# A two-layer decoder on one core: another order of the opening, filler products, casts on ScalarE, later clears, the last scaling on VectorE

## The chip, the cores and the metric

The kernel runs on one core of a Trainium2 chip, as one launch. The metric is the device time of an execution in microseconds; less is better. A core has five instruction queues: TensorE (PE: products and transposes), VectorE (DVE), ScalarE (ACT), GpSimd (POOL) and SyncE (SP, which here only issues transfers). Each works off its own list in order, and they wait for each other through semaphores.

## The reference, cut to what matters

The input x has shape (4, 512, 128), a context (4, 154, 128). Six blocks follow each other, each with a residual and a layer norm behind it:

```python
x = _layernorm(x + _L0_attn_ref(x, ...))        # 16 heads of 8, causal; q and k are layer-normed
x = _layernorm(x + _L0_xattn_ref(x, ctx, ...))  # 16 heads of 8 over the context
x = _layernorm(x + _L0_ffn_ref(x, ...))         # 8 experts, softmax gates of at least 0.1
x = _layernorm(x + _L1_attn_ref(x, ...))        # linear attention, chunks of 128
x = _layernorm(x + _L1_xattn_ref(x, ctx, ...))  # 8 heads of 128 over the context
x = _layernorm(x + _L1_ffn_ref(x, ...))         # gated, 384 hidden
```

The start of the first block is what the edits touch most: `qkv = x @ W_qkv`, q and k each normed over their 128 features (mean and variance), then scores q.k per head, a maximum per row, the exponentials.

## The kernel before, in words

The work is cut by batch (b = 0 to 3). A batch passes two "attention" blocks in turns of four heads (`TURNS`, line 78 on): a turn makes the scores `S` (the causal ones in five pieces), VectorE takes their maxima (`maxima`, L1783 and L1788), which are split into bf16 parts (L1800 to L1806), transposed (`mT`) and written by SyncE as extra rows beside q (L798); then the transposed scores `ST`, their exponentials on ACT (L1537) and the products with v (`PV`). The four blocks behind it (`rest_groups`) work on halves of a batch (h = 0, 1), in buffers called slots: z = 0 and 1 for batches 0 to 2, z = 2 and 3 for batch 3. Batches overlap: attention of one runs beside the rest of the one before.

Scores are exact to about f32 because q and k are split into three bf16 parts each (`parts`, first, second, third: rounded value, rounded remainder, remainder of that) and placed by transfers six times, each into rows of the 64-row contraction ("placing", `place_self`, L777 on SyncE; for the first batch half of them on ACT, `place_first`, L1457). The placings with third parts are all among ACT's. K and Q buffers (`Q6`, `K6`) must have been cleared before, which POOL does by memsets (L884 to L901): for batch 0 first, then K_1 (for cross attention), then, in `late_zeros`, the halves for batch 1, and VXR and vaug.

All engines walk one list of steps, `schedule()`. 16 streams of steps are merged by a written-out string, `MERGE`, one letter for each step or group; `BANK_OF` gives the PSUM bank of each step that needs one. Each engine does its part of a step, in the order of the list, so a step that stands earlier in the list stands earlier in each engine's queue. `takes` and `held_back` say which steps must stand ahead of which.

The steps of the opening, for a batch: `x0T` transposes x (L1051), ACT copies it (L1444); `qkv` makes four products of 128x384 (L1082), ACT copies each (L1485); `qk_moments` on VectorE (L1715, L1723); `qk_norm`: POOL takes the root of the variances (`root`, L945 and L948), then for batch 0 VectorE scales q (L1735) and ACT k (L1492), for later batches POOL both (L913); `qkT` transposes q, then k, ACT writes the first part (L1507), VectorE the remainder `left` (L1759), the second part (L1749) and the third (L1751); `place`. `wT` steps transpose the context and weights of later blocks. `xv` makes the values of the cross attention; VectorE adds their bias (L1882, L1887).

The norms of the rest: VectorE makes the moments (L1827, L1831), POOL the root and, in `shifted` (L953), minus mean times root; ACT scales (`norm`, L1663); step `store` sends the result out (L809).

## Time and profile before

| | |
|---|---|
| median of 3 runs | 491.82 us (491.47 to 494.59) |
| the profiled execution | 493.74 us |
| its span, first to last instruction | 491.9 us |
| busy, PE / DVE / ACT / POOL | 458.1 / 384.5 / 351.2 / 190.2 us |
| mean granted TensorE clock | 0.984 of full speed |

Busy times of the engines overlap. A row of the timeline or of the chain gives the start and the length in microseconds; "issue" is time in which an engine waited for nothing that the profile shows, among it the landing of transfers. The granted clock is given as a share of 2.4 GHz; 0.50 is 1.2 GHz. In the shares by line, PE has 74% of the chain that ended last and DVE 9%.

### The profile page before, as it was taken

To read this page: it belongs to the slowest core of one execution; us is meant where nothing else is said; L and a number is where in the kernel's file an instruction comes from. 1 tells how busy PE (TensorE), PEld (TensorE's weight loads), DVE (VectorE), ACT (ScalarE), POOL (GpSimd) and SP (SyncE) were. 2 spreads that over 40 slices of the span, in tenths; PEclk is the share of its full clock that TensorE was granted. 3 is DMA by queue.
4 is the path that set the end of the run, shared out by engine and by line. 5 is a ranking of instruction groups with operands and counts; after the bars stand their busy time and mean duration, and the time that the engine had idled before them with its cause. 6 is when DMAs were issued, how large, how long until landed. Compare 5 with 4: busy or idle time off the path is not lost.

```text
span 491.9 us, 12390 instructions
## 1 busy us (share of the span) xinstructions
PE 458.1 (93%) x4416; PEld 307.2 (62%) x4416; DVE 384.5 (78%) x1133; ACT 351.2 (71%) x893; POOL 190.2 (39%) x365
## 2 busy tenths in 40 slices
PE   5567989998999999999999999999999999999994
PEld 2344557655546546666778555658754756996894
DVE  3559998799899999997788888858788678554465
ACT  3326676866858769887776688986767878969743
POOL 8760001570101644344143232334414537646352
PEclk9689999999999999999999999999999999999999
DMA  7650310032300213001110000030000000000001
GB/s 240 152 148 4 105 31 25 4 86 73 88 4 23 66 39 85 17 2 26 35 35 21 6 3 2 4 88 4 2 13 13 0 2 1 1 2 1 1 1 43
DMA packets 27185, 18.40 MB, mean 37 GB/s; under 512 B 8217, under 2 KB 26773, under 8 KB 26997
## 3 DMA queue, kind: packets, MB, share of 16 engines
q1 hardware_dynamic: 23413, 15.44, 11.8%
q10 hardware_dynamic: 3712, 2.17, 1.7%
q8 instruction: 36, 0.59, 0.5%
q14 instruction: 24, 0.20, 0.1%
HBM read 5.58 MB, written 1.05 MB: 13 GB/s over the span
## 4 chain that ended last, share of the span: by engine, by line
PE 74%; DVE 9%; POOL 6%; issue 3%; ACT 3%; DMA 2%; SPq 2%; ACTq 0%; POOLq 0%; DVEq 0%
PE psum L1051 11%; PE psum L1372 6%; PE psum L1162 6%; PE psum L1395 6%; PE psum L1308 6%; PE psum L1103 5%; PE psum L1130 4%; DVE nmax L1788 4%; PE psum L1406 4%; PE psum L1152 3%; PE psum L1149 3%; PE psum L1417 2%; PE psum L1190 2%; PE psum L1082 2%; PE psum L1109 1%
## 5 line engine op out<-in xcount | busy, mean ns | idle before, releaser
L1537 ACT ACTIVATE EX<-psum 128x1024 f32<-128x1024 f32 (+1 forms) x128 | 118.5, 976 | 8.7 <-PE psum L1136 4.3
L1788 DVE TENSOR_REDUCE nmax<-psum 128x2 f32<-128x768 f32 (+1 forms) x96 | 77.5, 861 | 7.4 <-PE psum L1109 7.2
L1783 DVE TENSOR_REDUCE nmax<-psum 128x4 f32<-128x616 f32 (+1 forms) x80 | 68.1, 876 | 2.9 <-PE psum L1103 2.6
L1103 PE MATMUL psum<-K,Q 64*128 64x154 bf16 (+4 forms) x512 | 50.9, 268 | 5.9 <-issue 4.5
L1014 POOL TENSOR_TENSOR GP<-REST,xrs 128x512 f32<-128x512 f32 (+1 forms) x48 | 32.5, 700 | 41.4 <-DVE xrs L2025 27.6
L1130 PE MATMUL psum<-Q,K 64*128 64x512 bf16 (+3 forms) x320 | 44.7, 315 | 1.6 <-DVE nmax L1788 1.2
L1620 ACT ACTIVATE REST<-psum,nxmax 128x154 f32<-128x154 f32 x96 | 36.2, 395 | 10.7 <-DVE nxmax L2015 9.8
L1444 ACT COPY pvraw<-psum 128x512 f32<-128x512 f32 x32 | 18.7, 585 | 34.3 <-PE psum L1162 24.6
L1103 PEld LDWEIGHTS psum<-K,Q 64*128 64x128 bf16 x512 | 21.4, 95 | 28.2 <-issue 19.1
L1162 PE MATMUL psum<-EX,V 128*32 128x256 f32 (+3 forms) x512 | 37.8, 435 | 0.1
L945 POOL TENSOR_SCALAR rstd_rest<-moments_rest 128x2 f32<-128x2 f32 x32 | 7.3, 228 | 79.1 <-DVE moments_rest L1831 78.7
L2015 DVE TENSOR_REDUCE nxmax<-psum 128x2 f32<-128x308 f32 x64 | 28.7, 469 | 5.8 <-PE psum L1372 5.1
L1372 PE MATMUL psum<-GP,xT 128*128 128x308 f32 x96 | 30.3, 431 | 0.0
L1109 PE MATMUL psum<-maskS,ident 64*128 64x64 bf16 (+1 forms) x512 | 28.3, 207 | 0.0
L1109 PEld LDWEIGHTS psum<-maskS,ident 64*128 64x128 bf16 x512 | 23.8, 97 | 6.5
L1136 PE MATMUL psum<-maskT,ident 64*128 64x64 bf16 (+1 forms) x512 | 27.2, 203 | 0.0
L1136 PEld LDWEIGHTS psum<-maskT,ident 64*128 64x128 bf16 x512 | 22.9, 94 | 6.2
L1162 PEld LDWEIGHTS psum<-EX,V 128*32 128x32 f32 x512 | 14.5, 109 | 18.0 <-issue 16.9
L1395 PE MATMUL psum<-VM,REST 128*128 128x128 f32 x192 | 24.1, 278 | 0.3
L948 POOL TENSOR_TENSOR rstd_rest<-rstd_rest,power 128x2 f32<-128x2 f32 x32 | 22.9, 714 | 2.7
L926 POOL COPY V<-qkn 128x256 f32<-128x256 f32 x8 | 3.7, 461 | 51.9 <-PE psum L1162 51.9
L1395 PEld LDWEIGHTS psum<-VM,REST 128*128 128x128 f32 x192 | 22.4, 192 | 1.7 <-issue 1.1
(338 smaller groups left out, 1162.4 us busy)
## 6 DMA issues: line engine op xcount, KB each, us to landing
Q<-xparts SPq DMA_DIRECT2D x24, 128.0 KB
Q<-parts SPq DMA_DIRECT2D x21, 128.0 KB
K<-parts SPq DMA_DIRECT2D x21, 128.0 KB
X<-in_x SPq DMA_DIRECT2D x4, 256.0 KB, 3.6
Q<-in_L_xattn_Wkv SPq DMA_DIRECT2D x1, 1024.0 KB, 6.6
K<-xkparts SPq DMA_DIRECT2D x24, 38.5 KB
out<-XB_rest SPq DMA_DIRECT2D x6, 128.0 KB, 1.9
Q<-in_L_xattn_Wq SPq DMA_DIRECT2D x1, 512.0 KB, 4.4
```

The lines of the kernel that those rows point to most:

```text
L1051: last = nc.tensor.transpose(to[0:n, at:at + m], src, ident[0:m, 0:m])
L1103: last = mm(to[:, r, at:at + n], Q6[a][p, b % 2, 2 * g + jj, P * q:P * q + P], K6[a][p, b % 2, 2 * g + jj, 0:n], start=True, stop=bool(a))
L1109: last = mm(to[:, r, at + n - P + TILE * e:at + n], ident2[p, e, :], maskS[p, e, TILE * e:P], start=False, stop=e == 0)
L1130: last = mm(to[:, r, at:at + n], K6[a][p, b % 2, 2 * g + jj, P * k:P * k + P], Q6[a][p, b % 2, 2 * g + jj, P * k:S], start=True, stop=bool(a))
L1136: last = mm(to[:, r, at:at + TILE * (e + 1)], ident2[p, e, :], maskT[p, e, 0:TILE * (e + 1)], start=False, stop=e == 1)
L1162: last = mm(to[32 * h:32 * h + 32, P * k:S], V[:, k, 4 * g + h, :], EX[:, ex_slot(b, a, g, u) + h % 2, at:at + n], start=k == PV_ORDER[0], ...
L1372: fills_(mm(fill(key)[:, 0:2 * C], half_of(b, h).xT[4][:, P * q:P * q + P], G[:, head:head + 2, :].rearrange("p h c -> p (h c)")), key)
L1395: mm(to, of.XPT[:, head, :], VM[:, head, :], start=head == 0, stop=False)
L1537: drains(nc.scalar.activation(dst, src, ACT.Exp), key)
L1620: last = nc.scalar.activation(of.XE[:, i, :], src[:, C * j:C * j + C], ACT.Exp, bias=of.nxmax[:, i:i + 1], accum_out=of.xsum[:, i:i + 1])
L1783: last = vec.tensor_reduce(nmax[:, :, :, q], src[:, :, 0:2 * n].rearrange("p r (j k) -> p r j k", j=2), AX.X, ALU.max, negate=True)
L1788: last = vec.tensor_reduce(nmax[:, :, jj, q], src[:, :, at:at + P * (q + 1)], AX.X, ALU.max, negate=True)
```

## The change

What it does, part by part:

- The first product of the second batch must stand behind the last placing of the first (`takes`). `MERGE` and `BANK_OF` are new throughout: most steps move by a few places. Of the `wT` steps none stands ahead of the first scores any more, `xv` stands behind the scores of the fourth turn instead of ahead of those of the second.
- ACT makes the second parts of q and k for batch 0; for this the two remainders have buffers of their own, `left` and a piece of EX.
- POOL's clears of K_1 and its late clears stand behind the second batch's scalings.
- TensorE multiplies the identity by itself, six times ahead of the first transposes of x and twice ahead of the first qkv product; nothing reads the results.
- For batch 3 `shifted` is left out behind the root, and VectorE makes (Y - mean) * root in place of ACT, four times for each half.

```diff
@@ takes @@
     if what == "qkv":
-        return [(b, "x0T", 0)]
+        return [(b, "x0T", 0)] + ([(0, "place", 1, 1)] if b == 1 else [])
@@ MERGE: the order of the steps, by stream @@
-    "rrrrrrwurrrrwllrlruuurrlrsssssuuuuvsssusuttsstrrttsssspptssttttllpsssrpptsslltttstpu"
+    "rrrrrrrrrwrlwlllrrrsrrssuuuussruuuuuusssststtsrttssspptstststlrptsssspwplllttststtvu"
...
@@ BANK_OF: the PSUM bank of each step @@
-    "024613570246135062406234523046270460246250624064206245064206420624016247024602460123"
+    "024613570246124067160234523640264062046124602460246702402640642064523064204602460123"
...
@@ build @@
+        def first_left(w):
+
+            return EX[:, 0, :] if w else left[:, :]
@@ gpsimd @@
             pool.wait_ge(first_zeros_ready, 1)
-            step(nc.gpsimd.memset(words(K6[1].rearrange("p b h t -> p (b h) t")), 0.0))
-            step(nc.gpsimd.memset(K6[1].rearrange("p b h t -> p (b h) t").bitcast(F32)[
-                :, :, 0:C // 2], TWO_ONES))
 
             def late_zeros():
-                pool.wait_ge(qk_normed, 1)
+                step(nc.gpsimd.memset(words(K6[1].rearrange("p b h t -> p (b h) t")), 0.0))
+                step(nc.gpsimd.memset(K6[1].rearrange("p b h t -> p (b h) t").bitcast(F32)[
+                    :, :, 0:C // 2], TWO_ONES))
                 for w, value in enumerate((0.0, TWO_ONES)):
                     step(nc.gpsimd.memset(words((Q6, K6)[w][0][:, 1, :, :]), value))
@@ qk_norm @@
                 if b == 0:
-                    late_zeros()
                     return
...
                     last.then_inc(qk_normed, 1)
+                if b == 1:
+                    late_zeros()
@@ rest_root @@
-                step(root(of.rstd, of.moments, LN_EPS))
-                shifted(of.shift, of.moments, of.rstd, 2).then_inc(rest_rstd_ready[z], 1)
+                last = root(of.rstd, of.moments, LN_EPS)
+                if b < B - 1:
+                    step(last)
+                    last = shifted(of.shift, of.moments, of.rstd, 2)
+                last.then_inc(rest_rstd_ready[z], 1)
@@ tensor @@
+            def keep_busy(to, count):
+
+                for _ in range(count):
+                    mm(to[:, 0:P], ident[:, :], ident[:, :], start=True, stop=True)
@@ x_T @@
                 if n == 0:
+                    if b == 0:
+                        keep_busy(fill((0, "x0T", 0)), 6)
                     pe.wait_ge(x_loaded[b], 16)
@@ qkv @@
+                key = (b, "qkv", n)
                 if n == 0:
+                    if b == 0:
+                        keep_busy(fill(key), 2)
                     drained(pe, (b, "x0T", 0))
                     if b == 0:
                         pe.wait_ge(wqkv_ready, 1)
-                key = (b, "qkv", n)
@@ scalar: qkT @@
+                if b == 0 and w:
+                    for v in range(2):
+                        drained(act, (0, "qkT", v))
+                        copy(parts[:, v, 1, :], first_left(v)).then_inc(part_ready[0][1], 1)
@@ scalar: norm @@
+                if b == B - 1:
+                    return
                 z, of = slot(b, a), half_of(b, a)
@@ vector: qkT @@
-                drains(vec.scalar_tensor_tensor(left[:, :], bank(key),
+                rest = first_left(w) if b == 0 else left[:, :]
+                drains(vec.scalar_tensor_tensor(rest, bank(key),
                                                 col("k_scale") if w else col(QS),
                                                 parts[:, w, 0, :], ALU.mult, ALU.subtract), key)
-                drained(dve, key)
-                split(left[:, :], parts[:, w, :, :], part_ready[0], 2 * b + w + 1)
+                if b:
+                    drained(dve, key)
+                    split(rest, parts[:, w, :, :], part_ready[0], 2 * b + w + 1)
+                elif w:
+                    for v in range(2):
+                        dve.wait_ge(part_ready[0][1], v + 1)
+                        vec.tensor_tensor(parts[:, v, 2, :], first_left(v), parts[:, v, 1, :],
+                                          ALU.subtract).then_inc(part_ready[0][2], 1)
+                    splits.append((part_ready[0][2], 2))
@@ vector @@
-            work = {"qk_moments": qk_moments, "qk_norm": qk_norm, "qkT": qkT,
+            def last_norm(b, h, n=None):
+
+                if n is None or b < B - 1:
+                    return
+                z, of = slot(b, h), half_of(b, h)
+                dve.wait_ge(rest_rstd_ready[z], norms_until(b, n))
+                dst = of.XB if n == 5 else of.X[n + 1]
+                for i in range(2):
+                    last = vec.tensor_scalar(dst[:, i, :], of.Y[:, i, :], of.moments[:, i, 0:1],
+                                             of.rstd[:, i:i + 1], ALU.subtract, ALU.mult)
+                last.then_inc(rest_x_ready[z], 1)
+
+            work = {"norm": last_norm, "qk_moments": qk_moments, "qk_norm": qk_norm, "qkT": qkT,
```
The names in the rows of order are those of buffers; a number behind x is how many of a kind follow each other. ACT in the opening before, from its scaling of k on (L1492); L1444 copies x of the second batch, L1485 its products, L1553 the context, L1457 are placings, L1463 late loads:

```order
L1492 ACTIVATE qkn<-qkn,qkshift,qkrstd 128x128 x4
L1507 ACTIVATE parts<-psum,cols 128x512 x2
L1444 COPY xT<-psum 128x512
L1457 DMA Q_0<-parts 16x8x512 x3
L1485 COPY qkn<-psum 128x384 x2
L1553 COPY cT<-psum 128x154 x3
L1485 COPY qkn<-psum 128x384 x2
L1457 DMA K_0<-parts 16x8x512 x3
L1463 DMA gw<-in_L_ffn_gate_w 128x8
L1463 DMA gb<-in_L_ffn_gate_b 128x8
```

and in the changed kernel, from the second parts (L1528) on; L1460 copies x, L1473 are placings, L1479 late loads, L1501 copies the second batch's products:

```order
L1528 CAST parts<-left 128x512
L1528 CAST parts<-EX 128x512
L1460 COPY xT<-psum 128x512
L1473 DMA Q_0<-parts 16x8x512 x3
L1473 DMA K_0<-parts 16x8x512 x3
L1479 DMA gw<-in_L_ffn_gate_w 128x8
L1479 DMA gb<-in_L_ffn_gate_b 128x8
L1479 DMA ew<-in_L_ffn_expert_w 128x8x128
L1479 DMA REST<-in_L_ffn_w_gate 128x3x128
L1479 DMA REST<-in_L_ffn_w_up 128x3x128
L1479 DMA REST<-in_L_ffn_w_down 128x384
L1501 COPY qkn<-psum 128x384 x4
```

All six placings now stand ahead of the second batch's products, and the six late loads with them; the context's copies follow.

VectorE in the opening before, from the remainder of q on, to the first turn's maxima (L1788, L1783), their split and the additions for the cross values (L1882):

```order
L1749 CAST parts<-left 128x512
L1751 TENSOR_TENSOR parts<-left,parts 128x512
L1715 BN_STATS qkstats<-qkn 128x6 x8
L1723 BN_AGGR qkmoments<-qkstats 128x2 x8
L1788 TENSOR_REDUCE nmax<-psum 128x2 x6
L1783 TENSOR_REDUCE nmax<-psum 128x4
L1800 CAST mparts<-nmax 128x2x8
L1802 TENSOR_TENSOR nrest<-nmax,mparts 128x16
L1804 CAST mparts<-nrest 128x2x8
L1806 TENSOR_TENSOR mparts<-nrest,mparts 128x2x8
L1882 TENSOR_TENSOR VXR<-psum,rows 26x4x8 x4
L1887 TENSOR_TENSOR VX<-psum,rows 128x16x8
```

and in the changed kernel (L1791 makes the third parts, L1818 and L1813 are the maxima):

```order
L1791 TENSOR_TENSOR parts<-left,parts 128x512
L1791 TENSOR_TENSOR parts<-EX,parts 128x512
L1818 TENSOR_REDUCE nmax<-psum 128x2
L1737 BN_STATS qkstats<-qkn 128x6 x8
L1745 BN_AGGR qkmoments<-qkstats 128x2 x8
L1818 TENSOR_REDUCE nmax<-psum 128x2 x5
L1813 TENSOR_REDUCE nmax<-psum 128x4
L1830 CAST mparts<-nmax 128x2x8
L1832 TENSOR_TENSOR nrest<-nmax,mparts 128x16
L1834 CAST mparts<-nrest 128x2x8
L1836 TENSOR_TENSOR mparts<-nrest,mparts 128x2x8
L1818 TENSOR_REDUCE nmax<-psum 128x2 x6
```

One maximum now stands ahead of the second batch's moments and the other five behind; the cross values' additions are gone from between the turns.

VectorE at its end before, behind the last hidden blocks (L1862 adds the residual):

```order
L1862 TENSOR_TENSOR Q_0<-psum,Q_0 128x256
L1827 BN_STATS stats_rest<-Q_0 128x6 x2
L1831 BN_AGGR moments_rest<-stats_rest 128x2 x2
L1862 TENSOR_TENSOR K_0<-psum,K_0 128x256
L1827 BN_STATS stats_rest<-K_0 128x6 x2
L1831 BN_AGGR moments_rest<-stats_rest 128x2 x2
```

and in the changed kernel (L2113 is the scaling):

```order
L1892 TENSOR_TENSOR Q_0<-psum,Q_0 128x256
L1857 BN_STATS stats_rest<-Q_0 128x6 x2
L1861 BN_AGGR moments_rest<-stats_rest 128x2 x2
L1892 TENSOR_TENSOR K_0<-psum,K_0 128x256
L1857 BN_STATS stats_rest<-K_0 128x6 x2
L1861 BN_AGGR moments_rest<-stats_rest 128x2 x2
L2113 TENSOR_SCALAR parts<-Q_0,moments_rest,rstd_rest 128x128 x2
L2113 TENSOR_SCALAR parts<-K_0,moments_rest,rstd_rest 128x128 x2
```

Both scalings stand behind the second half's moments.

## Rows read from the trace of the kernel before

**Rows 1.** The chain of waits, 27 to 38 us; columns: start us, us, what.

```profile
27.14 4.51 issue
...
32.17 4.75 DVE nmax L1788 x6
36.92 1.14 DVE nmax L1783
```

**Rows 2.** Busy by stretch: from:to, PE, PEld, DVE, ACT, POOL; clock, DMA share, GB/s.

```profile
32.00:68.00 36.00, 31.11 (x501) 19.89 (x494) 34.76 (x65) 20.82 (x30) 5.71 (x8) 0.95 0.29 77
100.00:120.00 20.00, 18.09 (x287) 10.93 (x279) 18.27 (x39) 12.88 (x19) 7.68 (x10) 1.00 0.36 92
400.00:480.00 80.00, 78.47 (x502) 63.57 (x501) 47.91 (x175) 61.06 (x236) 44.02 (x89) 1.00 0.00 1
```

**Rows 3.** Timeline, up to q's transposes; columns: start us, us, what [idle before <-releaser].

```profile
1.14 0.29 POOL L848 TENSOR_SCALAR_AFFINE_SELECT ident<-REST 128x128 f32<-128x128 f32 x1
...
4.41 1.08 PE L1051 MATMUL psum<-ident,X 128*128 128x128 f32 x4 [4.41 <-DMA X<-in_x]
...
7.94 0.48 ACT L1485 COPY qkn<-psum 128x384 f32<-128x384 f32 x1 [1.83 <-PE psum L1082]
...
9.22 0.48 ACT L1485 COPY qkn<-psum 128x384 f32<-128x384 f32 x1 [0.80 <-PE psum L1082]
...
11.38 1.17 POOL L889 MEMSET K<- 128x1280 f32 x1
...
12.81 0.64 DVE L1723 BATCH_NORM_AGGREGATE qkmoments<-qkstats 128x2 f32<-128x6 f32 x8
...
14.29 0.25 POOL L945 TENSOR_SCALAR qkrstd<-qkmoments 128x8 f32<-128x8 f32 x1
...
16.40 1.11 DVE L1735 TENSOR_SCALAR qkn<-qkn,qkmoments,qkrstd 128x128 f32<-128x128 f32 x4
...
17.57 1.97 PE L1051 MATMUL psum<-ident,qkn 128*128 128x128 f32 x8 [5.50 <-DVE qkn L1735]
```

**Rows 4.** Timeline, ACT's last copies of the second batch's products.

```profile
26.54 0.48 ACT L1485 COPY qkn<-psum 128x384 f32<-128x384 f32 x1 [0.56 <-PE psum L1082]
27.18 0.48 ACT L1485 COPY qkn<-psum 128x384 f32<-128x384 f32 x1 [0.17 <-PE psum L1082]
```

**Rows 5.** Stretch of 0.2 us in which the granted clock rises.

```profile
25.20:25.40 0.20, 0.20 (x1) 0.00 (x0) 0.18 (x1) 0.20 (x1) 0.00 (x0) 0.60 1.06 200
```

**Rows 6.** Instructions on tile parts, 15 to 70 us; duration ns min/median/max.

```profile
L1507 ACT ACTIVATE parts<-psum,cols x4: 681/687/687, 18.7 to 56.7; 128x512 bf16<-128x512 f32 x4
L1759 DVE SCALAR_TENSOR_TENSOR left<-psum,cols,parts x4: 741/748/752, 19.4 to 58.1; 128x512 f32<-128x512 f32 x4
L1749 DVE CAST parts<-left x4: 426/548/1352, 20.2 to 58.8; 128x512 bf16<-128x512 f32 x4
L1751 DVE TENSOR_TENSOR parts<-left,parts x4: 693/694/767, 21.6 to 59.3; 128x512 bf16<-128x512 f32 x4
...
L1457 ACTq DMA_DIRECT2D K<-parts x3: 540/610/612, 27.2 to 28.5; - x3
```

**Rows 7.** VectorE's timeline between the first and second turn.

```profile
38.80 0.78 DVE L1882 TENSOR_TENSOR VXR<-psum,rows 26x32 f32<-26x32 f32 x4
...
39.80 4.74 DVE L1788 TENSOR_REDUCE nmax<-psum 128x2 f32<-128x1024 f32 x6
```

**Rows 8.** Timeline, second batch: POOL's scalings and SyncE's placings of q.

```profile
31.05 6.23 POOL L913 TENSOR_SCALAR qkn<-qkn,qkmoments,qkrstd 128x128 f32<-128x128 f32 x8
...
48.71 3.89 SPq L777 DMA_DIRECT2D Q<-parts  x6
```

**Rows 9.** Timeline, the last normalization.

```profile
486.70 0.25 DVE L1831 BATCH_NORM_AGGREGATE moments_rest<-stats_rest 128x2 f32<-128x6 f32 x2
...
488.15 0.50 POOL L953 TENSOR_SCALAR shift_rest<-moments_rest,rstd_rest 128x1 f32<-128x1 f32 x2
488.69 0.88 ACT L1663 ACTIVATE parts<-K,shift_rest,rstd_rest 128x128 f32<-128x128 f32 x2 [1.02 <-POOL shift_rest L953]
```

40 lines of the change are left out of this document (20 added, 20 removed).

## Prediction

> **What bounds the kernel now.** I read the chain of waits first, then the busy table by stretches, then the timeline of the opening and of the end. In the chain the reader is to see that the opening is latency and not work: TensorE waits 4.51 us with nothing that the profile names, up to 31.65, and from 32.17 the chain runs through VectorE's maxima of the first self-attention turn, 4.75 and 1.14 us, to 38.06 [rows 1]. The stretches then tell who sets the pace: from 32 to 68 us VectorE is busy 34.76 of 36 us (97%) and TensorE 31.11; from 100 to 120 neither is full (18.09 and 18.27 of 20); from 400 to 480 TensorE is busy 78.47 of 80 and VectorE only 47.91 [rows 2]. So a microsecond counts in full in the opening, on VectorE until about 68, and behind TensorE's last product; on TensorE's side of the middle only its idle time can go. The edits lie in the opening and at the end; between them the order is new throughout, which I cost apart.
>
> **Opening, up to the first transposes of q.** Two things stand before 14.29, when POOL starts the roots: VectorE's moments, which end at 12.81 + 0.64 = 13.45, and POOL's own queue, where two clears of K_1 (from 11.38) and a copy of V stand ahead of the root [rows 3]. The change puts these three behind the root, so POOL is free at about 11.35. The moments then decide, and they hang on the four products of the first batch. ACT's copies of them start at 7.94 and 9.22, 1.28 us apart [rows 3], while the last two of the second batch are 0.64 us apart (26.54, 27.18) [rows 4]. The first four thus ran at 1.2 GHz and the later ones at 2.4. The granted clock rose between the two batches' products, at 25.3 (mean 0.60 over 25.2 to 25.4, 0.50 before it and 1.00 behind) [rows 5].
>
> The change lets TensorE multiply the identity once it is written (1.14 + 0.29 = 1.43) [rows 3]: six products, each four times 128 columns at 1.2 GHz, 0.43 us by the scale of the 384-column product (1.28 / 3), so 2.6 us, over before x lands at 4.41. Two more (0.86 us) stand between x's transposes, which end at 5.49 [rows 3], and the first product: over by 6.35, when that product, copied from 7.94 after 1.28 us of its own, could hardly have begun. If the clock is up by 6.3 to 8 us, the four products save between 1.6 and 2.56 us, and the moments end at 10.9 to 11.9; with POOL free at 11.35 I take the root at 11.6 instead of 14.29, 2.7 us earlier. If the clock stays low, the moments end at 13.45 as now and the gain is 0.8. These are the ends.
>
> The Trainium skill ("TensorE: Matmul & The Clock Gate", Part 1) says that the array warms up by the time it is kept active, not by the number of products, and that the point shifts from run to run with the same kernel. By that rule the filler earns up to the 2.56 us, but not the same in every execution; by the rows of the opening alone it could earn nothing. The rest goes without this sentence.
>
> From root to q's transposes nothing changes (17.57 - 14.29 = 3.28 us [rows 3]): q is transposed from 14.9.
>
> **Opening, from there to the first scores.** The last thing the scores waited for was ACT's placing of k: ACT copied the second batch's products first, to 27.66 [rows 4]; its three issues start at 27.2 to 28.5, 0.61 us each, so they ended at 29.1 [rows 6], and TensorE started 2.55 us behind them. In the changed order nothing lies ahead of them but the second batch's x. Step by step from 14.9: q transposed to 15.95 (as x, 1.08), first parts on ACT to 16.75 and, of k, 17.6 (0.69 each and a hand-over); VectorE's rests to 17.5 and 18.35 (0.75 each); ACT's two casts, to 18.2 and 19.0 (0.6 each: between VectorE's 0.43 and ACT's own 0.69 for a scaled write); VectorE's two differences to 19.8 (0.69 each) [rows 3, 6]. ACT copies x to 19.6, issues six placings at 0.61 us to 23.3, and the scores start at 25.9, 5.75 us earlier. SyncE's placings need less (no third parts) and its queue is free of loads before.
>
> Not all of it arrives. ACT then still issues its six late loads (0.6 each, as its placings) to 26.9, and only now copies the second batch's products (0.49 each, the fourth to 28.85). VectorE has one maximum at 26.4 and stands behind it in order for the moments of the second batch: last two statistics 0.49, aggregates 0.64 [rows 3], so 30.0 (the 0.49 put like a copy's). The other maxima take 4.75 us [rows 1] and end at 34.7 against 38.06 now: 3.35 us. Behind the split of the maxima (0.75 us: 38.06 to 38.80), at 35.5, VectorE now goes on with the additions for the cross values (38.80 to 39.80 [rows 7]); in the changed order nothing lies there, and it waits for TensorE's transpose and the next scores, which I put at 0.8 us (by the 0.5 us from scores to maximum at 32.17, and 0.3 for the transpose and its hand-over), and starts at 36.3 against 39.80 [rows 7]. The 1.0 us of additions is still to be done at a later place of the stretch in which VectorE is the bound. The opening so gives 3.5 - 1.0 = 2.5 us. Its bounds: 0.6 if the clock stays low (1.9 less), 3.5 if the additions find a gap.
>
> **Late clears.** POOL now clears K_1, the second halves of Q and K, VXR and vaug only behind the second batch's normalization: some 7640 columns, at 1.17 us for K_1's 1280 [rows 3] 7.0 us, and with five small ones 7.7. The root at 30.0 takes 2 us and the eight scalings behind it 6.23 [rows 8], so this is 38.2 to 45.9; SyncE's placings of the second batch went out only from 48.71 [rows 8], so the wait is covered. What isn't covered is VectorE's work on SBUF in these 8 us: one cast of 512 columns and the small splits. By the row the slowest cast of the first batch, which ran while POOL cleared, lost 0.92 us against the fastest (1.35 - 0.43) [rows 6]; bounds 0 and 1.8, taken 0.3, since maxima read PSUM and fill most of the time. The Trainium skill ("SBUF — State Buffer", Who interferes with whom) says that GpSimd and such a cast lock one pair of ports for a whole instruction. By this rule the cast that comes behind the start of a clear waits until its end, up to 1.8 us; by the row, half of that. The trace agrees in kind.
>
> **End.** In the last batch the multiplication by -1 of mean and root on POOL goes, and the scaling moves from ACT to VectorE. The last one: shift 488.15 to 488.65, ACT 488.69 to 489.57. VectorE scaled four blocks in 1.11 us [rows 3], so two in 0.6: 488.1 to 488.7, 0.9 us less [rows 9]. The other seven are shorter too, by some 0.9 us each, but TensorE has only 1.53 us of idle time in 400 to 480 [rows 2]: I take 0.5 of it, bounds 0 and 1.5.
>
> **The sum.** 2.5 - 0.3 + 0.9 + 0.5 = 3.6 us. The profiled execution took 493.74 us (span 491.9 and 1.8 around it), so it would be 490.1; the median shown is 491.82, 0.4% lower, so the forecast is 488.2. The new order between 60 and 480 us goes in at nothing: on TensorE there is nothing to win where it is full.
>
> **Rivals.** (a) The filler does not raise the clock in time. For it: the first products show no rise, and the filler leaves TensorE idle for 0.4 us before x lands. Against: it did rise at 25.3, behind the work that begins at 17.57. The opening gives 0.6: 491.82 - 0.6 + 0.3 - 1.4 = 490.1. The filler would then not do what it is said to do.
> (b) The new order closes gaps besides: VectorE's 1.2 us in 32 to 68 and TensorE's 1.9 us in 100 to 120 [rows 2], where placings of the cross attention are late. With 3 us of these: 485.2. For it: the spreads and placings of later batches stand at other places. Against: the order alone doesn't say which way.
> (c) VectorE stands waiting at the end. Each scaling now stands right behind its aggregates in VectorE's queue, and the root takes 1.1 us (486.95 to about 488.1) [rows 9]: six times before 480, 6.6 us in which no maximum of the other halves' cross attention is taken. If TensorE waits for all of it, 0.5 is lost and 6.6 added: 488.2 + 7.1 = 495.3, slower than before. It decides once TensorE's idle time in the 80 us before its end grows beyond 1.5 + 3.6 us. Against: VectorE is free 32 of 80 us there [rows 2].
>
> **Chances.** Forecast 0.50, (a) 0.15, (b) 0.30, (c) 0.05. The forecast's own range is 486.5 to 490.0; with (b) below and (a) above, and one more microsecond for the run's spread (491.47 to 494.59 before), 484.3 to 491.8; (c) lies outside. One per cent is 4.9 us, about what a measurement can tell from no change: below 486.9 lie most of (b) and a tenth of the forecast, 0.37; above 496.7 only the end of (c), 0.02.
>
> **What would show it.** Right: qkv copies of the first batch 0.64 apart; root of the first batch at 11.3 to 12; first scores at 25 to 26.5; first turn's last maximum at 34 to 35.5; last store issued 0.9 us behind the last root's end. Wrong: copies 1.28 apart (a); a first turn ended before 33, or TensorE idle under 1 us in 100 to 120 (b); TensorE idle over 5 us in its last 80 (c); a first score that waits for SyncE's placings, which I put ahead of ACT's.

## The result, and the profile after

The changed kernel takes 496.36 us (median of 16 runs, 494.39 to 497.14), the kernel before, run beside it, 493.27 (16 runs, 491.47 to 495.93): ratio 1.0045 with the interval 1.0028 to 1.0062, so 2.2 us slower, where 3.6 us of gain were forecast. (The two medians differ by 3.1 us. Sizes in this document go by the ratios and their intervals; medians can differ from them by up to 1 us.) The profiled execution took 497.09 us (span 495.4 against 491.9, mean granted clock 0.982 against 0.984).

The opening is where the forecast looked first, and up to the first scores it nearly holds. The changed kernel's timeline (start us, us, what):

```profile
7.49 0.48 ACT L1501 COPY qkn<-psum 128x384 f32<-128x384 f32 x1 [1.60 <-PE psum L1098]
...
9.42 0.48 ACT L1501 COPY qkn<-psum 128x384 f32<-128x384 f32 x1 [0.17 <-PE psum L1098]
10.45 0.64 DVE L1745 BATCH_NORM_AGGREGATE qkmoments<-qkstats 128x2 f32<-128x6 f32 x8
11.43 0.25 POOL L949 TENSOR_SCALAR qkrstd<-qkmoments 128x8 f32<-128x8 f32 x1
...
13.55 1.28 DVE L1757 TENSOR_SCALAR qkn<-qkn,qkmoments,qkrstd 128x128 f32<-128x128 f32 x4
...
14.88 1.33 PE L1063 MATMUL psum<-ident,qkn 128*128 128x128 f32 x5 [5.49 <-DVE qkn L1757]
...
16.03 0.69 ACT L1523 ACTIVATE parts<-psum,cols 128x512 bf16<-128x512 f32 x1 [0.72 <-PE psum L1063]
...
17.75 0.43 SPq L767 DMA_DIRECT2D cols<-in_L_attn_bv  x1
18.30 1.93 SPq L781 DMA_DIRECT2D Q<-parts  x3
...
20.62 2.10 ACTq L1473 DMA_DIRECT2D K<-parts  x3
...
27.59 0.61 PE L1119 MATMUL psum<-K,Q 64*128 64x512 bf16 x2 [3.83 <-issue]
28.39 1.23 DVE L1818 TENSOR_REDUCE nmax<-psum 128x2 f32<-128x1024 f32 x1 [8.66 <-PE psum L1125]
31.21 0.64 DVE L1745 BATCH_NORM_AGGREGATE qkmoments<-qkstats 128x2 f32<-128x6 f32 x8
...
35.27 1.21 DVE L1813 TENSOR_REDUCE nmax<-psum 128x4 f32<-128x1024 f32 x1
```

The four copies are 0.64 us apart (9.42 - 7.49 = 1.93 for three), half of the spacing in [rows 3]: the products ran at twice the rate. Only the spacing tells this, since the granted clock of the profile reads 1.00 in the first 10 us of both kernels. The root starts at 11.43 (forecast 11.6), q's transposes at 14.88 (14.9), ACT's last placing is issued by 22.72 (23.3). Then the forecast parts: the first score is at 27.59 and not at 25.9, the moments of the second batch at 31.21 + 0.64 and not at 30.0, and the first turn's last maximum ends at 36.48: 1.6 us ahead of [rows 1], not 3.35.

One reading of the prediction fails here: that SyncE's queue is free of loads before its placings. Q's first part is written at 16.72 (16.03 + 0.69), but SyncE issues loads until 18.18 and its first placing only at 18.30. In the kernel before, its queue was empty at 17.79 and the part came at 19.41. The first score follows this issue from trace to trace: with the changed opening and the filler it starts at 26.35 to 26.61 us where SyncE's first placing went out at 16.97 to 17.32 (three kernels), and at 27.07 to 27.59 where it went out at 17.55 to 18.30 (seven). No run moved these loads.

The stretches of the changed kernel (from:to length, PE, PEld, DVE, ACT, POOL, granted clock, DMA share, GB/s), first in the wait for the placings, then those of [rows 2]:

```profile
22.00:24.00 2.00, 1.75 (x3) 0.34 (x1) 0.00 (x0) 0.00 (x0) 0.00 (x0) 0.52 1.13 225
24.00:26.00 2.00, 0.00 (x0) 0.00 (x0) 0.00 (x0) 0.00 (x0) 0.00 (x0) 1.00 1.12 234
...
28.00:30.00 2.00, 2.00 (x10) 0.78 (x8) 1.60 (x4) 0.29 (x2) 0.00 (x0) 0.50 1.16 297
...
32.00:68.00 36.00, 28.50 (x451) 18.28 (x451) 32.63 (x61) 21.34 (x33) 16.02 (x21) 0.95 0.18 47
100.00:120.00 20.00, 17.50 (x272) 10.44 (x266) 17.84 (x44) 14.36 (x21) 8.99 (x13) 1.00 0.21 54
400.00:480.00 80.00, 78.21 (x516) 63.02 (x516) 51.10 (x193) 58.67 (x231) 41.12 (x78) 1.00 0.01 2
```

The transfer engines are full (a share above 1) from 20 us until the scores start, and TensorE, which idled for 3.8 us, is granted the half clock just as its scores begin. Behind 32 us both engines do less than before in the same stretch (PE 28.50 against 31.11, DVE 32.63 against 34.76), and in 100 to 120 again (17.50 against 18.09). The end, from the last aggregates (start us, us, what):

```profile
490.87 0.25 DVE L1861 BATCH_NORM_AGGREGATE moments_rest<-stats_rest 128x2 f32<-128x6 f32 x2
...
492.41 0.60 DVE L2113 TENSOR_SCALAR parts<-K,moments_rest,rstd_rest 128x128 f32<-128x128 f32 x2 [0.41 <-POOL rstd_rest L952]
```

Aggregates to the last scaling's end take 2.14 us, against 2.87 in [rows 9]: 0.73 gained, 0.9 forecast.

**Three stretches.** Both orders have worked off the same steps at two places: ahead of the transposes of the fifth turn's maxima, which are the 102nd of the 1031 steps in both, and (but for one step) ahead of those of the 32nd turn. The third part of these maxima's split on VectorE marks both in any trace. Before, then changed:

```profile
72.96 0.18 DVE L1806 TENSOR_TENSOR mparts<-nrest,mparts 128x16 bf16<-128x16 f32 x1
...
371.07 0.18 DVE L1806 TENSOR_TENSOR mparts<-nrest,mparts 128x16 bf16<-128x16 f32 x1
```

```profile
75.17 0.17 DVE L1836 TENSOR_TENSOR mparts<-nrest,mparts 128x16 bf16<-128x16 f32 x1
...
376.59 0.18 DVE L1836 TENSOR_TENSOR mparts<-nrest,mparts 128x16 bf16<-128x16 f32 x1
```

The difference of 3.5 us in span is thus +2.2 up to the fifth turn, +3.3 between, -2.0 behind. The forecast had -2.2, 0 and -1.4 in these places. The experiments take the three apart.

### The profile page after: what moved, and what is told of

It reads as the page before. It is cut to its first block, busy times and chain, and to the rows that moved or that the text cites. A ratio compares the mean times of both kernels' runs of the same rounds, so it can differ in the third digit from the quotient of the medians.

```text
span 495.4 us, 12408 instructions
## 1 busy us (share of the span) xinstructions
PE 461.3 (93%) x4432; PEld 309.7 (63%) x4432; DVE 388.0 (78%) x1147; ACT 345.3 (70%) x879; POOL 187.0 (38%) x349
## 4 chain that ended last, share of the span: by engine, by line
PE 73%; DVE 7%; POOL 5%; ACT 4%; SPq 4%; issue 3%; DMA 2%; POOLq 0%; ACTq 0%; DVEq 0%
PE psum L1063 10%; PE psum L1178 7%; PE psum L1324 6%; PE psum L1411 6%; PE psum L1119 6%; PE psum L1388 5%; PE psum L1146 4%; SPq L795 3%; PE psum L1422 3%; PE psum L1168 3%; DVE nmax L1818 3%; PE psum L1165 3%; PE psum L1206 2%; ACT EX L1557 2%; PE psum L1125 2%
## 5 line engine op out<-in xcount | busy, mean ns | idle before, releaser
L1818 DVE TENSOR_REDUCE nmax<-psum 128x2 f32<-128x768 f32 (+1 forms) x96 | 77.3, 860 | 14.2 <-PE psum L1125 13.9
L1813 DVE TENSOR_REDUCE nmax<-psum 128x4 f32<-128x616 f32 (+1 forms) x80 | 67.7, 875 | 5.6 <-PE psum L1119 5.5
L1119 PE MATMUL psum<-K,Q 64*128 64x154 bf16 (+4 forms) x512 | 49.5, 267 | 7.9 <-issue 3.8
L1146 PE MATMUL psum<-Q,K 64*128 64x512 bf16 (+3 forms) x320 | 43.6, 316 | 3.2 <-DMA Q<-mrows 1.3
L1460 ACT COPY pvraw<-psum 128x512 f32<-128x512 f32 x32 | 18.7, 584 | 33.4 <-PE psum L1178 26.7
L1178 PE MATMUL psum<-EX,V 128*32 128x256 f32 (+3 forms) x512 | 39.5, 451 | 0.5 <-ACT EX L1557 0.5
L949 POOL TENSOR_SCALAR rstd_attn<-moments_attn 128x4 f32<-128x4 f32 x8 | 1.9, 239 | 80.0 <-DVE moments_attn L1861 80.0
L1152 PE MATMUL psum<-maskT,ident 64*128 64x64 bf16 (+1 forms) x512 | 27.2, 203 | 0.0
L1146 PEld LDWEIGHTS psum<-Q,K 64*128 64x128 bf16 x320 | 15.1, 94 | 17.3 <-issue 9.5
```

The source lines that it names most:

```text
L1119: last = mm(to[:, r, at:at + n], Q6[a][p, b % 2, 2 * g + jj, P * q:P * q + P], K6[a][p, b % 2, 2 * g + jj, 0:n], start=True, stop=bool(a))
L1146: last = mm(to[:, r, at:at + n], K6[a][p, b % 2, 2 * g + jj, P * k:P * k + P], Q6[a][p, b % 2, 2 * g + jj, P * k:S], start=True, stop=bool(a))
L1152: last = mm(to[:, r, at:at + TILE * (e + 1)], ident2[p, e, :], maskT[p, e, 0:TILE * (e + 1)], start=False, stop=e == 1)
L1178: last = mm(to[32 * h:32 * h + 32, P * k:S], V[:, k, 4 * g + h, :], EX[:, ex_slot(b, a, g, u) + h % 2, at:at + n], start=k == PV_ORDER[0], ...
L1813: last = vec.tensor_reduce(nmax[:, :, :, q], src[:, :, 0:2 * n].rearrange("p r (j k) -> p r j k", j=2), AX.X, ALU.max, negate=True)
L1818: last = vec.tensor_reduce(nmax[:, :, jj, q], src[:, :, at:at + P * (q + 1)], AX.X, ALU.max, negate=True)
```

## The experiments

All were timed in five rounds beside the kernel before. This table is worked out from the split rows of each profiled execution, as above: the three stretches in us, then the time at the half clock in the first 60 us (from the granted clock of stretches of 10 us; it reads 1.00 in the first stretch of every kernel, so the half rate of the very first products isn't in it), and the ratio to before in the timed runs.

| kernel | to 5th turn | 5th to 32nd | to the end | half clock | ratio (interval) |
|---|---|---|---|---|---|
| before | 73.1 | 298.1 | 120.7 | 13.6 | 1 |
| changed | 75.3 | 301.4 | 118.6 | 17.2 | 1.0045 (1.0028 to 1.0062) |
| early_clears | 71.9 | 301.1 | 118.4 | 13.6 | 1.0044 (1.0019 to 1.0070) |
| no_filler | 76.6 | 301.1 | 118.5 | 17.2 | 1.0074 (1.0050 to 1.0098) |
| old_order_later | 73.6 | 297.2 | 123.9 | 10.4 | 1.0068 (1.0039 to 1.0097) |
| new_order_later_only | 72.8 | 301.0 | 133.3 | 13.6 | 1.0292 (1.0236 to 1.0348) |
| loads_behind | 75.7 | 300.7 | 118.6 | 23.8 | 1.0026 (1.0002 to 1.0049) |
| best_mix | 75.0 | 297.2 | 119.2 | 27.4 | 0.9979 (0.9953 to 1.0004) |
| best_mix2 | 73.5 | 297.5 | 119.1 | 17.2 | 0.9976 (0.9956 to 0.9996) |
| tail_only | 71.5 | 298.0 | 122.4 | 13.6 | 0.9973 (0.9942 to 1.0003) |
| opening_only | 74.9 | 297.3 | 120.6 | 23.8 | 0.9989 (0.9963 to 1.0016) |
| late_clears_only | 79.2 | 298.2 | 120.6 | 20.6 | 1.0159 (1.0121 to 1.0197) |
| mid1_new | 71.5 | 300.3 | 120.8 | 10.2 | 1.0044 (1.0011 to 1.0077) |
| mid2_new | 74.5 | 298.6 | 118.5 | 23.8 | 0.9984 (0.9960 to 1.0008) |
| mid1a_new | 72.1 | 300.4 | 120.9 | 13.6 | 1.0040 (1.0013 to 1.0066) |
| mid1b_new | 75.3 | 300.0 | 119.2 | 20.4 | 1.0017 (0.9991 to 1.0043) |
| mid1_undone | 74.1 | 298.9 | 118.7 | 27.2 | 0.9961 (0.9943 to 0.9980) |
| undone_behind | 74.1 | 298.7 | 118.5 | 27.2 | 0.9981 (0.9957 to 1.0006) |
| cover_wait | 74.5 | 301.4 | 118.6 | 17.0 | 1.0024 (1.0005 to 1.0044) |
| filled_gap | 76.7 | 297.3 | 119.2 | 20.4 | 0.9993 (0.9968 to 1.0018) |

The first column moves from run to run with the clock (71.5 to 75.3 over the seven kernels with before's opening), so one trace can't price the opening. The second is steady to some 0.7 us for a given order and opening, and so is the third but where the clock fell in it.

**The late clears, put early.** The changed kernel, with the six clears right behind the V copies of the first batch:

```diff
                     ).then_inc(v_spread, 1)
+                if b == 0 and y:
+                    late_zeros()
@@
-                if b == 1:
-                    late_zeros()
```

> The changed kernel with one edit: POOL's late clears (K_1, second halves of Q and K, VXR, vaug) stand behind the first batch's copies of V, from about 14.3 us to 22, and not behind the second batch's scalings. Theory 1 (the clears are the loss): in the changed kernel a cast of 128x16 took 1.57 us beside the clear of K instead of 0.17, and TensorE, idle for 2.24 us behind it, was granted half clock from 47.8 to 51.2 us and took 4.05 us for the next 32 products with v instead of 2.36. With the clears gone from there: no such cast over 0.4 us, split of the second turn's maxima done at about 45.1 instead of 46.6, of the third turn's at about 54 instead of 56.9, and 2 to 3.5 us less in all than the changed kernel: 492.8 to 494.4, the ratio to before 0.999 to 1.002. Theory 2 (the new order behind the opening is the loss): third turn earlier, but less than 1 us of it is left at the end: ratio 1.003 or more.

The trace shows what the late clears do to VectorE. The changed kernel, then the one with early clears (start us, us, what):

```profile
44.80 1.57 DVE L1834 CAST mparts<-nrest 128x16 bf16<-128x16 f32 x1
...
44.54 1.80 POOL L899 MEMSET K<- 128x2048 f32 x1
```

```profile
44.60 0.17 DVE L1834 CAST mparts<-nrest 128x16 bf16<-128x16 f32 x1
```

A cast of 16 columns that takes 0.17 us took 1.57 and ended with the clear, and TensorE waited 2.24 us for the split. Of the seven kernels with late clears and the changed opening four had this cast at 1.5 us or more (in the others no cast of this split took over 0.51), of the five with early clears none. But the ratios put nothing on it, 1.0044 against 1.0045, though their intervals leave room for over 1 us. And early clears are not free of the collision, they only move it: now POOL clears beside VectorE's scaling of q, on which q's transposes wait. Early_clears, then filled_gap (further down):

```profile
13.51 2.02 DVE L1757 TENSOR_SCALAR qkn<-qkn,qkmoments,qkrstd 128x128 f32<-128x128 f32 x4
...
13.53 3.10 DVE L1759 TENSOR_SCALAR qkn<-qkn,qkmoments,qkrstd 128x128 f32<-128x128 f32 x4
```

In all five kernels with early clears this scaling takes 2.02 us or more, in all seven with late ones at most 1.28. The transposes start at 15.59 and 16.68 us here, against 14.88 in the changed kernel. So this run compares two places of a collision, and doesn't price the late one.

Of the 3.4 us by which the first stretches differ here, a part is the clock, which fell again at 47.8 us in the one trace and not in the other; and the traced execution with early clears, 493.18 us, was among the fastest two of its twelve (median 495.92). Theory 1 is missed by the time; theory 2's ratio of 1.003 or more came.

**Before's order behind step 101, and the changed order behind it.** Both cut the list of steps where the orders agree:

```diff
-MERGE, BANK_OF: the changed ones
+old_order_later: steps 1 to 101 as changed, the rest as before; all other edits kept
+new_order_later_only: the kernel before, with its steps from 102 on in the changed order
```

> The changed kernel, but from the 102nd step of the list on in the order and the banks of before; up to there the two orders hold the same steps. Theory 1 (late clears): the loss of the first three turns stays (+1.9 us at the split of the third turn against before), and the end stays within 1 us of the changed kernel less the last scaling's gain: ratio 1.003 to 1.005. Theory 2 (the new order costs behind the opening): the difference to before, which in the changed kernel grows from +1.6 us at the seventh turn's split to +3 to +4 from the tenth on and +5.5 at the last, stays at about +1.6 to +2.5, and with the shorter end (0.9 us) the kernel is at +0.5 to +1.5 us: ratio 1.001 to 1.003.

> The kernel before with nothing changed but the order and banks from the 102nd step on, which are those of the changed kernel; no filler, no casts on ACT, clears as before, last scaling on ACT. Theory 1: same as before within 1 us, ratio 0.998 to 1.002. Theory 2: 1.5 to 3.5 us slower than before, ratio 1.003 to 1.007.

Both kernels were slower than either theory allowed (1.0068 and 1.0292). The middle follows the order: 297.2 with before's, 301.0 with the changed one. The opening adds little, 0.8 us: before's order takes 298.0 to 298.2 behind before's opening and 297.2 to 297.5 behind the changed one. The tail follows order and norms together. VectorE's norms in before's order cost 3.2 us (123.9 against 120.7), ACT's norms in the changed order 12.7 (133.3). The waits of the latter's tail (engine line, waited for: us in total, times, longest):

```profile
POOL rstd_rest L945 <- DVE moments_rest L1831: 31.9, 13, 9.6
DVE nxmax L2015 <- PE psum L1372: 10.3, 5, 8.9
```

POOL's roots wait for VectorE's moments. I read this so, without a run that shows it: each order was made for the engine that scales in it, and puts what must not be late behind the other engine's work.

**No filler.** `keep_busy` and its two calls taken out.

```diff
-                        keep_busy(fill((0, "x0T", 0)), 6)
-                        keep_busy(fill(key), 2)
```

> The changed kernel without the eight products of the identity by itself. If the filler raised the clock (copies of the first batch's products 0.64 us apart in the changed kernel, 1.28 before), they are 1.28 apart here, POOL starts the root of the first batch at 13.5 instead of 11.4, the first scores come 2 us later, and of that some 1.5 to 2 us are left at the end: ratio 1.007 to 1.009. Rival (the opening's gain is not kept, since the placings wait for the transfers and not for their issue): first scores less than 1 us later and the end the same: ratio 1.003 to 1.006.

The filler is worth its forecast in kind: without it the kernel is slower by 0.0029 of the time of before, 1.4 us by ratios measured apart (the intervals overlap a little), and 1.3 in the first stretch. The root is 2.0 us later (13.44 against 11.43), as expected, but the first score only 0.8 (28.41 against 27.59), as the rival had it: SyncE's first placing goes out at 18.82, only 0.5 later than with the filler.

**Late loads behind the placings.** ACT's six loads moved behind its copies of the second batch's products.

```diff
                 if w:
-                    load(late)
@@ qkv
+                if b == 1 and n == NB - 1:
+                    load(late)
```

> The changed kernel, but ACT issues the six late loads (1.1 MB, at 22.75 to 26.9 us) only behind its copies of the second batch's products, so behind 27 us, and the twelve placings (1.5 MB) have the DMA engines alone. Theory that the placings are held by the loads that share the engines with them (DMA share 1.09 to 1.18 from 20 to 30 us): first score product at 26.0 instead of 27.6, turn 0 about 1.5 us earlier than in the changed kernel, and the copies of the second batch's products at 23.5 instead of 27.0. Rival, that the placings' own traffic sets it (their packets are small): score product within 0.4 us of 27.6, turn 0 within 0.4. Time: 495.0 by the theory if the gain of the opening is carried on, 496.4 by the rival, and 498 if the loads now arrive in the way of the exponentials that ACT owes from 38 us on.

The first score starts at 27.29, only 0.3 us sooner, which is less than it moves between traces with the loads in place (26.54 to 27.59). The stretch just ahead of it is full without the loads:

```profile
24.00:26.00 2.00, 0.00 (x0) 0.00 (x0) 0.00 (x0) 0.08 (x1) 0.00 (x0) 1.00 1.12 236
26.00:27.00 1.00, 0.00 (x0) 0.00 (x0) 0.00 (x0) 0.00 (x0) 0.00 (x0) 0.62 0.26 52
```

So the rival holds: the late loads don't set the time, the placings' own traffic does. The transfer engines are full with the placings alone until just past 26 us, and the score starts 1 us behind. Twelve of 128 KB are 1.57 MB, at 236 GB/s 6.7 us. Before, this traffic lay in two parts with a pause between them: nine of the twelve had landed, and the last three were alone.

**Mixed kernels.** Both take the changed opening, early clears, before's order from step 102 to 834 and the changed order and norms behind it; the second has the late loads behind too.

```diff
-MERGE, BANK_OF: the changed ones
+steps 1 to 101 and 835 to 1031 as changed, 102 to 834 as before
```

> The changed kernel with three of its parts as they are (opening, the first 101 steps of its order, the last norms on DVE with its own order behind step 834, so behind about 372 us), but the late clears right behind the V copies, and the order between step 101 and 834 that of the kernel before. Theory that the late clears cost some 3 us and the new order of the middle some 3: turn 31 at -1.5 to -3 against before, end -3.5 to -5, time 489.5. Rival, that the order of the middle only passes on what the opening does (the lead is lost at whichever order): turn 31 within 0.7 of before, time 492.5.

> As the mixed kernel, and the late loads behind ACT's copies of the second batch's products as well. Theory of the shared DMA engines: 1 to 1.5 us earlier than the mixed kernel at turn 0 and at the end, time 488.5. Rival, that the placings are not held by the loads: same as the mixed kernel within 0.3.

Against early_clears, of which the first differs in the middle alone, it is 0.0065 faster, 3.2 us by the ratios (2.4 by the medians, from runs on two chips), and 3.9 in the middle of the traces: the loss of the middle is real in both.

The 489.5 and 488.5 us that the theories gave were missed: the middle came back, the opening brought nothing. The second mixed kernel equals the first (0.9976 and 0.9979), as its rival said.

**One part alone on the kernel before.** The tail (norms on VectorE, changed order from step 835), the opening (with early clears), the clears:

```diff
+tail_only: last_norm on DVE, rest_root without shift for batch 3; steps 835 to 1031 as changed
+opening_only: casts on ACT, filler, early clears; steps 1 to 101 as changed
+late_clears_only: the clears of K_1 and late_zeros() behind the second batch's scalings
```

> The kernel before with one part of the change alone: the last batch's seven norms on DVE without their shift on POOL, and the changed kernel's order behind step 834 (about 372 us). Up to turn 31 it is before. Theory (the new tail with DVE's norms gains what the profile of the changed kernel shows behind turn 31): end -2.0, time 491.5, the span behind turn 31 shorter by 1.8 to 2.3. Rival, that the gain there comes from the lead or lag with which the tail is entered: end within 0.5 of before, 493.4.

> The kernel before with the opening of the change alone (order of the first 101 steps, ACT's casts, the filler on TensorE) and the clears right behind the V copies; its order behind step 101 and its last norms on ACT are those of before. Theory from the medians so far (the mixed kernel and the one with the new tail alone differ by 1.0 us in the wrong direction): the opening is worth nothing, time within 0.8 of before. Rival, my forecast of 2.5 us in the opening: ratio 0.995, 491.6 where before is 494.1; a third reading, half of it as the profile of the changed kernel shows at turn 0 (1.2): 0.9975.

> The kernel before with only the clears moved: K_1's and the five late ones on POOL behind the second batch's scalings. Theory from the profile of the changed kernel (a cast of DVE held from 0.17 to 1.57 us beside the clears, TensorE waiting 2.2 us and a half clock behind it): turn 2 at +1.5 to +3 against before, and what is left at turn 31 is the same; time +1.5. Rival, from the medians of the changed kernel with early and with late clears, which are equal (1.0044 and 1.0045): time within 0.5 of before, a delay at turn 2 of under 0.5.

The tail alone: 0.9973, 1.3 us, with an interval that just holds 1. Its traced tail was longer than before's (122.4 against 120.7), and the clock fell in it, behind a gap of 1.76 us in TensorE's work (from:to length, PE, PEld, DVE, ACT, POOL, clock, DMA share, GB/s):

```profile
394.00:396.00 2.00, 0.65 (x6) 0.68 (x6) 0.53 (x3) 1.41 (x5) 1.45 (x4) 1.00 0.00 0
396.00:403.00 7.00, 6.98 (x38) 5.11 (x37) 3.75 (x20) 2.50 (x8) 0.00 (x0) 0.52 0.01 2
```

Where it did not fall, this tail took 118.4 to 119.2, 1.5 to 2.3 us less than 120.7. The opening alone is worth nothing that can be measured. The clears alone cost 7.9 us, where 1.5 or nothing was expected, and that is a wait (waits of TensorE in 32 to 100 us):

```profile
PE psum L1246 <- POOL vaug L900: 8.2, 1, 8.2
```

In before's order the cross values' product (L1246), which needs VXR and vaug cleared, stands ahead of the second turn's scores; the changed order has it behind those of the fourth. The late clears can't be had with before's order of the opening.

**Halving the middle.** On the kernel with the new tail alone, the changed order in one part of the middle; and the changed kernel with one part undone.

```diff
+mid1_new: steps 102 to 425 as changed      (about 73 to 207 us)
+mid2_new: steps 426 to 834 as changed      (about 207 to 372 us)
+mid1a_new: steps 102 to 201 as changed     (about 73 to 123 us)
+mid1b_new: steps 202 to 425 as changed     (about 123 to 207 us)
+mid1_undone: the changed kernel, steps 102 to 425 as before
```

> The kernel before with the new tail (as in the run of the tail alone) and the changed kernel's order between step 101 and 425, so between turn 4 and 18 (about 73 to 207 us). Theory that the new order costs most around the placings of the cross-attention (100 to 125 us): turn 19 and later 2.0 us behind where the run of the tail alone has it relative to turn 4, and this difference constant from there to turn 31; time 494.3. Rival, that the cost sits in the second half: less than 0.7 here.

> The same with the changed kernel's order between step 425 and 834 alone (about 207 to 372 us). Theory: 1.0 us behind at turn 31, none of it before turn 19; time 493.4. Rival, the cost sits here: over 2 us at turn 31.

> The kernel before with the new tail, and the changed kernel's order between step 101 and 201 alone (turns 4 to 9, about 73 to 120 us, with the first cross-attention's placings). Theory of one wait: the whole 2.3 us are lost here, between turn 4 and turn 10, and the rest of the trace is parallel to the run with the new tail alone; time 494.8 where that run is 492.5. Rival, many small gaps in the whole stretch: 1.0 us lost here, time 493.5.

> The same with the changed kernel's order between step 201 and 425 alone (turns 10 to 18, about 123 to 207 us). Theory of one wait: within 0.3 us of the run with the new tail alone at turn 20. Rival: 1.3 us behind it at turn 20, time 493.8.

> The changed kernel with one thing undone: the order between step 101 and 425 is that of before (opening, late clears, the rest of the order and the norms are the change's). Theory that this stretch carries the whole loss: ratio to before 0.998, 493.1. Rival, that the late clears need the new order here (before's order asks for the cleared tiles sooner): turn 1 to 4 over 2 us behind before, time 495.5.

The first half costs 2.3 us of trace (300.3 against 298.0) and 0.0071 of time (1.0044 against 0.9973), the second 0.6 and 0.0011. Undone in the changed kernel it turns 1.0045 into 0.9961: **this kernel beats both**, by 1.9 us against before in this measurement. It is the best of nineteen, and a near twin (undone_behind, below) came to 0.9981 with an interval that holds 1, so the true gain may well be smaller. Its rival, that before's order would stand waiting for the late clears, fell: cleared tiles are first asked for in the 101 steps that stay as changed.

The theory of one wait is not borne out: it had 2.3 us in mid1a_new and at most 0.3 in mid1b_new, and the middles cost 2.4 and 2.0. Inside the first half, mid1a_new loses 2.2 us between the fifth and the tenth turn and 0.3 behind. Its trace, then that of the new tail alone, in stretches of 8 us:

```profile
96.00:104.00 8.00, 7.52 (x129) 4.24 (x128) 7.78 (x25) 5.51 (x9) 6.85 (x9) 1.00 0.31 79
104.00:112.00 8.00, 6.80 (x96) 4.31 (x97) 6.21 (x14) 4.76 (x10) 2.85 (x5) 1.00 0.21 56
112.00:120.00 8.00, 6.69 (x99) 3.67 (x100) 7.49 (x19) 5.44 (x9) 0.00 (x0) 1.00 0.11 22
120.00:128.00 8.00, 6.83 (x63) 3.97 (x64) 6.25 (x20) 5.86 (x10) 0.40 (x1) 1.00 0.52 143
```

```profile
96.00:104.00 8.00, 7.95 (x126) 4.59 (x121) 7.22 (x22) 5.75 (x8) 7.66 (x10) 1.00 0.37 96
104.00:112.00 8.00, 7.14 (x99) 4.45 (x100) 7.50 (x14) 5.24 (x10) 2.11 (x4) 1.00 0.32 80
112.00:120.00 8.00, 6.92 (x101) 4.02 (x99) 7.46 (x20) 4.97 (x9) 0.88 (x1) 1.00 0.24 65
120.00:128.00 8.00, 7.80 (x70) 4.29 (x69) 7.24 (x21) 6.53 (x10) 2.24 (x6) 1.00 0.45 118
```

TensorE is idle 4.16 us in these 32 against 2.19: 2.0 us more. One wait has a name. In mid1a_new a write of maxima stands on SyncE between the two halves of K's placings, and the scores that wait for Q's stand right behind (start us, us, what):

```profile
95.83 1.87 SPq L791 DMA_DIRECT2D K<-xkparts  x3
97.79 0.77 SPq L798 DMA_DIRECT2D Q<-mrows  x1
98.67 1.82 SPq L791 DMA_DIRECT2D K<-xkparts  x3
100.62 4.12 SPq L791 DMA_DIRECT2D Q<-xparts  x6
...
107.88 0.44 PE L1106 MATMUL psum<-K,Q 64*128 64x154 bf16 x8 [0.98 <-DMA Q<-xparts]
...
108.23 1.51 DVE L1788 TENSOR_REDUCE nmax<-psum 128x4 f32<-128x616 f32 x2 [1.55 <-PE psum L1106]
```

In the kernel with the new tail alone SyncE issues Q's from 99.89, and VectorE has a split of the third batch's q in that place, from 106.69 to 108.62.

**Covering that wait.** The changed kernel, with the third batch's scaling and q transposes (steps `qk_norm`, `qkT`) two places sooner:

```diff
-mT(1,0,3), S(0,1,0,0), S(0,1,0,1), qk_norm(2), qkT(2,0)
+mT(1,0,3), qk_norm(2), qkT(2,0), S(0,1,0,0), S(0,1,0,1)
```

> The changed kernel with two steps moved by two places: the key and query placing's transposes of the third batch and their split on DVE (1.9 us) stand ahead of the first two scores of the cross-attention, so that DVE has work while TensorE waits for Q's placings (1.0 us on TensorE and 1.55 us on DVE in the trace). Theory that this wait is the loss of the stretch: turns 8 to 12 earlier by 1.5 us and the end as well, time 494.5 where the changed kernel is 496.4 (ratio 1.0008). Rival, many small gaps, of which this is one that closes itself: under 0.5 us at turn 12.

TensorE's wait for Q's placings (1.0 us) went, and another came (waits of VectorE, 73 to 125 us):

```profile
DVE left L1782 <- ACT parts L1523: 1.5, 1, 1.5
```

The middle stays at 301.4. So the loss is not this wait: closing this gap opened another. That the rest is spread in the same way is likely, but not shown. The 0.0021 between this kernel and the changed one, within both intervals, lies in the first column if anywhere.

**The late loads once more.** The kernel mid1_undone with the edit of loads_behind:

```diff
-                    load(late)          (behind place_first)
+                    load(late)          (behind the second batch's qkv copies)
```

> The changed kernel with before's order between step 101 and 425 (which is faster than before, 0.9961) and the late loads behind ACT's copies of the second batch's products. Theory of the shared DMA engines: first score 0.5 us sooner, as between the two mixed kernels, time 0.3 less, ratio 0.9955. Rival: no difference within the interval.

No difference that can be told (0.9981 and 0.9961, the intervals overlap): the late loads cost nothing that these runs can tell. The second measurement of nearly the same kernel is also a warning on the first: 0.0020 lie between them.

**Filling the gap ahead of the scores.** The second mixed kernel with ten more identity products:

```diff
                 if a == b == u == g == 0:
                     pe.wait_ge(consts_ready, 1)
+                    fill((b, "S", a, g, u))
+                    keep_busy(pair((b, "S", a, g, u))[:, 0, :], 10)
```

> The second mixed kernel (new opening, early clears, late loads behind, before's order in the middle, new tail) with ten more multiplications of the identity on TensorE in the 2.9 us in which it waits for the placings, ahead of the first score. Theory that the half clock gives back what the opening gains: no fall of the granted clock between 24 and 35 us, turn 2 at -2 or better against before, time 491.5 where the second mixed kernel is 493.4. Rival, that the fall comes whatever TensorE does there, or the added work delays the first scores: within 0.5 of the second mixed kernel.

The timeline and two stretches:

```profile
25.35 3.32 PE L1053 MATMUL psum<-ident 128*128 128x128 f32 x20
28.60 0.39 PE L1121 MATMUL psum<-K,Q 64*128 64x512 bf16 x2
```

```profile
28.00:30.00 2.00, 2.00 (x17) 1.10 (x17) 0.88 (x1) 0.04 (x1) 0.00 (x0) 1.00 0.00 0
34.00:36.00 2.00, 0.97 (x16) 0.81 (x18) 0.87 (x3) 0.86 (x4) 1.89 (x3) 0.53 1.09 315
```

The clock was full under the first scores, as wanted, but they began at 28.60 and not at 27.07, and the fall at 34, which the second mixed kernel has too (0.50 in 34 to 36, 1.00 in 38 to 40), now lasted beyond 40. It comes behind a stretch in which TensorE has little to do (0.43 of 2 us busy in 32 to 34). Not all of the later start is the filler's: ahead of it ACT's placings of k had gone out 1.0 us later than in the second mixed kernel (22.27 against 21.30), behind the scaling of q that took 3.10 us and not 2.02. Nothing gained (0.9993 against 0.9976).

## Why the prediction was wrong

The prediction said 488.2 and gave a range of 484.3 to 491.8; the median is 496.36, outside, and the side is the other. Between 3.6 us of gain and 2.2 of loss lie 5.8: by the columns of the table 3.0 of them are in the middle, 3.5 in the opening and late clears (forecast -2.2, by the traces +1.3), and the end gave 0.7 more than forecast.

1. **The step that failed: "The new order between 60 and 480 us goes in at nothing: on TensorE there is nothing to win where it is full."** There was something to lose. The middle costs 2.6 to 3.3 us against before in every trace with the changed order, and 3.9 us or 0.0065 of the time in the pair that differs in it alone, most of it in steps 102 to 425. I bounded this cost only from the side of gain, rival (b), although [rows 2] showed 1.9 us of idle time on TensorE and 1.7 on VectorE in 100 to 120: two engines at 90% that feed each other through placings, where a shift can open a gap. The rival for the slow side, (c), looked at the end instead, where the new order gains. Its 495.3 us lie near the 496.36 measured, but by luck: its sign was TensorE idle for over 5 us in the last 80, and in 400 to 480 it is idle 1.8.

2. **The landing of the placings (2.55 us behind the last issue) was mis-sized.** It came from a state in which nine of the twelve placings had landed before. All twelve in one go need 6.7 us of full transfer engines: 4.9 us behind the last issue. The landing took 2.3 us longer than put, the last issue came 0.6 sooner, so the first score is 1.7 us later than forecast, and that is nearly all of the 1.8 us by which the first turn falls short of its 3.35. The other part of this step is SyncE's queue, read as free.

3. **The clock.** I priced the filler and the emptied queue of POOL together, 2.7 us at the root, and that came out within 0.2 us: 2.86, of which the filler is 2.0 (11.43 against 13.44 without it). But the first turn of [rows 1] is one draw: the seven kernels with before's opening and clears start their first score anywhere from 29.70 to 33.09 us (31.2 on average; 29.70 to 29.76 where the granted clock was full in 22 to 24 us, later where it was 0.50), the ten with the changed opening and the filler at 26.35 to 27.59 (27.1). Of these 4.1 us 1.0 is left at the first turn's split (37.6 against 38.6), and at the fifth turn it is a loss. The half clock goes the same way: over those seven kernels it lasts 15.5 us of the first 60 on average and the fifth turn ends at 73.0; over those ten (filled_gap left out) 20.5 us and 74.3 (73.8 over the four with early clears, 74.6 over the six with late ones). In the timed runs of opening_only the mean granted clock is 0.9774, beside 0.9803 of before. Of the 1.3 us by which the fifth turn is behind, 0.8 come back by the 32nd turn in before's order (297.3 against 298.1). That the clock takes the gain is what these averages suggest; no run fixed the clock, and filled_gap, which tried to hold it, only moved the fall.

4. **"Late clears", 0.3 us with bounds 0 and 1.8.** The mechanism was right: a small cast was held for 1.4 us until the clear beside it ended, where I read 0.92 from [rows 6]. The trace agrees with the rule cited from the Trainium skill ("SBUF — State Buffer", Who interferes with whom): the wait lasts until the clear is over. What it costs in the whole was not measured: early_clears gives the same ratio, but has the collision in another place. What I hadn't seen is that the clears need the new order: alone they cost 7.9 us.

5. **End: 0.9 forecast, 0.73 measured.** "The other seven, 0.5": the tail as a whole gained 1.5 to 2.3 us instead of 1.4. But it is no property of the norms: in before's order they cost 3.2. I costed the edit and the order apart, and they have a price only together.

By the columns of the table (first: averages, +1.3; middle: 301.1 on average with the changed order and opening, +3.0; last: -2.1) the change should cost 2.2 us, which is what was measured. That it fits so well is partly luck: the first column moves by up to 3.8 us between traces of one opening, and opening_only, timed, came out level (0.9989).

**What stays open:** which gaps make up the 2.0 us between 96 and 128 us, since the one that was covered came back elsewhere, and why mid1a_new and mid1b_new cost 2.4 and 2.0 apart and 2.3 together. How much of the opening's loss is the clock was not settled. The PSUM banks (`BANK_OF`) were swapped together with the order in every experiment, so the middle's loss belongs to the two together.
